# A decoder layer on one core: block 0's choice of experts ahead of the barrier, weight splits at other blocks, blocks turned a step ahead, last products ahead of row moments

## What is computed

```python
logits = x.astype(jnp.float32) @ gate_w.astype(jnp.float32).T
scores = jax.nn.softmax(logits, axis=-1)
topk_w, topk_idx = jax.lax.top_k(scores, K)
topk_w = topk_w / (topk_w.sum(-1, keepdims=True) + 1e-20) * RSF
capacity = math.ceil(CF * N * K / E)
pos = jnp.cumsum(one_hot, axis=0) - 1
...
eo = jnp.einsum('nei,ehi->neh', jax.nn.silu(g) * u, we_down)
y = jnp.einsum('neh,ne->nh', eo, comb)
sh = jax.nn.silu(x @ ws_gate.T) * (x @ ws_up.T) @ ws_down.T
```

## Time and profile before

| | |
|---|---|
| median of 3 runs | 1394.81 us (1392.65 to 1396.25) |
| profiled execution, its own time | 1398.77 us |
| its span | 1397.0 us |
| TensorE busy in the span | 1309.3 us (94%) |
| VectorE | 1078.8 us (77%) |
| ScalarE | 925.5 us (66%) |
| GpSimd | 456.2 us (33%) |
| mean granted TensorE clock | 0.975 |

### The profile page before, as it was taken

One profiled execution on the slowest core, in us unless ns is written; L12 is line 12 of the kernel. 1 busy time (PEld: TensorE's weight loads), 2 busy tenths in 40 slices (PEclk: granted clock), 3 DMA queues, 4 the chain that ended last, 5 costly groups with the idle time before them and its releaser, 6 DMA issues. The chain is left out here.

```text
span 1397.0 us, 27271 instructions
## 1 busy us (share of the span) xinstructions
PE 1309.3 (94%) x8312; PEld 776.9 (56%) x8312; DVE 1078.8 (77%) x2227; ACT 925.5 (66%) x1776; POOL 456.2 (33%) x487
## 2 busy tenths in 40 slices
PE   3999999999999999999999999999968999999995
PEld 2534454444444444444544445443546799999984
DVE  5889789888978887897898888889577745555566
ACT  3387767777777776776677677778655645565555
POOL 3334203301511330151133020111146636666662
PEclk8699999999999999999999999999999999999998
DMA  5554434334424433442443444242056447777694
GB/s 166 135 167 129 125 126 141 104 119 142 134 68 135 145 95 115 143 140 79 129 138 94 138 124 132 78 135 73 17 184 207 170 142 134 135 156 146 136 185 132
DMA packets 110089, 181.47 MB, mean 130 GB/s; under 512 B 20368, under 2 KB 67600, under 8 KB 105872
## 3 DMA queue, kind: packets, MB, share of 16 engines
q1 hardware_dynamic: 90576, 155.70, 36.6%
q0 software_dynamic: 18816, 23.60, 9.7%
q10 hardware_dynamic: 576, 0.79, 0.3%
HBM read 99.67 MB, written 79.30 MB: 128 GB/s over the span
## 5 line engine op out<-in xcount | busy, mean ns | idle before, releaser
L802 ACT ACTIVATE prob<-ps_sc 128x512 f32<-128x512 f32 x1024 | 551.3, 601 | 195.0 <-PE ps_sc L1064 194.1
L847 DVE TENSOR_REDUCE nm<-ps_ring 128x1 f32<-128x512 f32 x1024 | 638.5, 679 | 53.0 <-PE ps_ring L1049 52.5
L1049 PE MATMUL ps_ring<-qk 48*128 48x512 f32 x1024 | 408.6, 471 | 11.9 <-DMA qk<-hbm_self 7.1
L1064 PE MATMUL ps_sc<-qk 50*128 50x512 f32 x1024 | 389.8, 454 | 10.7 <-ACT prob L802 9.6
L1064 PEld LDWEIGHTS ps_sc<-qk 50*128 50x128 f32 x1024 | 161.5, 187 | 301.5 <-ACT prob L802 215.7
L1081 PE MATMUL ps_out<-prob,va 128*32 128x512 f32 x2048 | 276.8, 613 | 1.6 <-ACT ot L678 0.7
L1902 PE MATMUL ps_gu<-x2f,we 128*128 128x256 f32 (+1 forms) x1320 | 214.9, 317 | 3.2 <-ACT sg L1524 2.3
L1902 PEld LDWEIGHTS ps_gu<-x2f,we 128*128 128x128 f32 x1320 | 183.8, 191 | 17.1 <-ACT sg L1524 3.2
L1049 PEld LDWEIGHTS ps_ring<-qk 48*128 48x128 f32 x1024 | 167.1, 189 | 43.2 <-DVE nm L847 27.2
L1902 PE MATMUL ps_dn<-we,hf 128*128 128x256 f32 x864 | 115.6, 285 | 7.1 <-DVE hf L1766 7.1
L607 POOL TENSOR_TENSOR rstd<-mv,eps 128x2 f32<-128x2 f32 x32 | 6.3, 197 | 345.9 <-DVE mv L935 345.9
(11 more groups left out here) (182 smaller groups left out, 1578.6 us busy)
## 6 DMA issues: line engine op xcount, KB each, us to landing
qk<-hbm_cross SPq DMA_DIRECT2D x384, 64.0 KB, 2.3
qk<-hbm_self SPq DMA_DIRECT2D x372, 64.0 KB, 2.3
hbm_self<-stage SPq DMA_DIRECT2D x16, 1024.0 KB, 3.9
hbm_cross<-stage SPq DMA_DIRECT2D x16, 1024.0 KB, 4.1
slots_x<-zeros SPq DMA_DIRECT2D x8, 1360.0 KB, 5.9
xs<-slots_x SPq DMA_DIRECT2D x40, 272.0 KB, 3.2
weraw<-w_moe SPq DMA_DIRECT2D x11, 768.0 KB, 4.7
xin<-x SPq DMA_DIRECT2D x9, 512.0 KB, 4.0
```

The costliest lines, as they stand in the source:

```text
L802: nc.scalar.activation(prob[:, s % 2, j, :], ps_sc[:, score_bank(h.cur, HG * s + j), :], ACT.Exp, scale=HD ** -0.5).then_inc(exp_done[a], 1)
L847: nc.vector.tensor_reduce(nm[:, g % 2, r:r + 1], bank(slot), axis=AX.X, op=ALU.max, negate=True).then_inc(max_done[a], 1)
L1049: nc.tensor.matmul(bank(slot), qk[rows, 0, pair, P * c:P * c + P], qk[rows, 1, pair, :], start=True, stop=True).then_inc(smax_done[a], 1)
L1064: nc.tensor.matmul(ps_sc[:, score_bank(inst, n), :], qk[rows, 1, h // 2, P * c:P * c + P], qk[rows, 0, h // 2, :], start=True, stop=True). ...
```

## The change

1. Block 0's choice. `choose` becomes a function for both phases (`choose_experts`), and block 0's is called at the end of VectorE's list of the attention phase. For that, block 0's logits come from `first_score` at step 4 of `post`, into bank 3 of `ps_gu`, and are turned at step 8 into the same bank; `first_block(0, 0)` moves from step 4 to 8, `(0, 1)` from 8 to 10. ScalarE copies the logits at step 5, and makes the exponential at step 13, between two pairs of row normalisations. The second block's up product, `first_block(1, 1)`, needs bank 3 and waits for VectorE's read of it.
2. Weight splits. Splits 1, 2 and 3 (second shared expert, routed experts 0 and 1) stood at blocks 0 to 2 on ScalarE and 1 to 3 on VectorE. Now split 1 stands at block 5 on ScalarE and 6 on VectorE, splits 2 and 3 behind jobs 8 and 9. The loads of weights follow: number 3 behind block 6's store, numbers 4 and 5 behind the first chunk loads.
3. Turns. The first half of a block's turn is made a block sooner: block i+2 at the down products of block i-1, instead of block i+1 at the head of block i; `x_hi` and `x_lo` of that half move as well, ahead of the exponential and ahead of `choose`.
4. Tail. Moments 5 stand behind job 14 and moments 6 behind job 15's two products and low halves; normalisations 4 to 6 behind the silu of job 15.

The core of the diff:

```diff
+                    if h.name == "post" and s == 5:
+                        act.wait_ge(products_done, 1)
+                        nc.scalar.activation(by_expert[:, :], ps_gu[0:NE, 3, :], ACT.Copy).then_inc(kept_done, 1)
+                    if h.name == "post" and s == 13:
+                        act.wait_ge(shift_done, 1)
+                        nc.scalar.activation(r32[:, 1, :, :], r32[:, 0, :, :], ACT.Exp).then_inc(rexp_done, 1)
...
             every_period(dve, half)
+            choose_experts(dve, nc.vector, 0, ps_gu[:, 3, 0:TT * NE].rearrange("p (t e) -> p t e", t=TT), r4, r32, choice,
+                           idx[:, 0, :, :], sel, logits_done, shift_done, rexp_done, step_done)
...
                 if (c, kind) == (0, 0):
-                    pe.wait_ge(lo_done["c"], upto("c", GATE, 0))
-                    pe.wait_ge(lo_done["xt"], upto("xt", B, 1))
                     pe.wait_ge(exp_done[CROSS], B * NMAX)
-                    pe.wait_ge(oev_done[CROSS], B * NG)
+                if (c, kind) == (1, 1):
+                    pe.wait_ge(shift_done, 1)
...
                     if h.name == "post" and s == 4:
+                        first_score()
+                    if h.name == "post" and s == 8:
                         first_block(0, 0)
-                    if h.name == "post" and s == 8:
+                        first_logits()
+                    if h.name == "post" and s == 10:
                         first_block(0, 1)
-                    if h.name == "post" and s == 10:
                         first_block(1, 0)
                         first_block(1, 1)
-                        first_logits(owners)
...
-MOMENTS_AT = {(12, 0): 0, (12, 1): 1, (13, 0): 2, (13, 1): 3, (14, 0): 4, (15, 0): 5, (15, 1): 6}
-NORM_AT = {(12, 1): 0, (13, 0): 1, (13, 1): 2, (14, 0): 3, (14, 1): 4, (15, 1): 5}
+MOMENTS_AT = {(12, 0): 0, (12, 1): 1, (13, 0): 2, (13, 1): 3, (14, 0): 4, (14, 1): 5}
+NORM_AT = {(12, 1): 0, (13, 0): 1, (13, 1): 2, (14, 0): 3}
...
-                if i < 3:
-                    sp.wait_ge(w_lo, i + 2)
-                    load_weights(i + 3, EXPERTS[i + 3])
+                if i == 6:
+                    sp.wait_ge(w_lo, 2)
+                    load_weights(3, EXPERTS[3])
...
             for g in range(NCH - 1):
                 load_chunk(g, g)
+            for n in (4, 5):
+                sp.wait_ge(w_lo, n - 1)
+                load_weights(n, EXPERTS[n])
...
             for i in range(B):
-                if AHEAD <= i + 1 < B:
-                    x_hi(i + 1, 0)
                 gate(i, 0)
...
                 h_hi(i, 1)
+                if AHEAD <= i + 2 < B:
+                    x_hi(i + 2, 0)
...
-                if 1 <= i + 1 < 4:
-                    split_hi(i + 1, (i + 1) % 2, (i + 1) // 2 + 1)
+                if i == 5:
+                    split_hi(1, 1, 1)
 
             for j in range(B, LATE):
                 for c in range(IC):
                     gate(j, c)
                     h_hi(j, c)
                 keep(j - 1)
+                n = j - B + 2
+                split_hi(n, n % 2, n // 2 + 1)
...
+            for c in range(IC):
+                gate(NJ - 1, c)
+            norm(B - 4)
+            for c in range(IC):
+                h_hi(NJ - 1, c)
+            keep(NJ - 2)
+            norm(B - 3)
             norm(B - 2)
...
-                if 1 <= i < 4:
-                    split_lo(i, i % 2, i)
+                if i == 6:
+                    split_lo(1, 1, 1)
+                if AHEAD <= i + 2 < B:
+                    x_lo(i + 2, 0)
                 if i + 1 < B:
                     choose(i + 1)
...
+            for c in range(IC):
+                product(NJ - 1, c)
+            for c in range(IC):
+                h_lo(NJ - 1, c)
+            moments(B - 2)
             last_moments()
...
+            def turn_ahead(i):
+                pe.wait_ge(kept_done, i)
+                turn(i, 0)
...
             down(0)
+            turn_ahead(AHEAD)
             count(1)
...
                 down_pair(i - 1, 0)
+                if i + 2 < B:
+                    turn_ahead(i + 2)
                 if i + 1 < B:
                     turn_logits(i + 1)
                 down_pair(i - 1, 1)
```

More of the change, by code:

```diff
@@ L291, in attention_phase @@
     expert_rooms, block_rooms, raw_rooms = rooms
-    ident, wg, wgraw, idx, tok, spare, by_expert = held
-    gu_done, products_done, kept_done, logits_done = made
+    ident, wg, wgraw, idx, tok, spare, by_expert, r4, r32, choice, sel = held
+    gu_done, products_done, kept_done, logits_done, shift_done, rexp_done, step_done = made
     ps_gu, _, ps_t = banks
@@ L1194, in rooms_ahead, with wide, make_step, step @@
         return [ctx.enter_context(nc.sbuf_tensor(name, [P] + ROOMS[name], F32 if name == "weraw" else F32R)) for name in ROOMS]
+def wide(a):
+    return a.to_broadcast([P, TT, NE])
+def make_step(eng, step_done, i, done):
+    def step(ins):
+        done[0] += 1
+        ins.then_inc(step_done, 1)
+        eng.wait_ge(step_done, i * ROUTE_STEPS + done[0])
+    return step
+def choose_experts(eng, v, i, logits, r4, r32, choice, number, sel, logits_done, shift_done, rexp_done, step_done):
+    mx, total_e, inv, top1, j1, top2, j2 = (r4[:, k, :, :] for k in range(7))
+    shifted, e, s, eq, cand, rest = (r32[:, k, :, :] for k in range(6))
+    one, two = (choice[:, c, :, :] for c in range(2))
+    done = [0]
+    step = make_step(eng, step_done, i, done)
+    eng.wait_ge(logits_done, i + 1)
+    step(v.tensor_reduce(mx, logits, axis=AX.X, op=ALU.max))
+    v.tensor_tensor(shifted, logits, wide(mx), ALU.subtract).then_inc(shift_done, 1)
+    eng.wait_ge(rexp_done, i + 1)
+    step(v.tensor_reduce(total_e, e, axis=AX.X, op=ALU.add))
+    step(v.reciprocal(inv, total_e))
+    step(v.tensor_tensor(s, e, wide(inv), ALU.mult))
+    step(v.tensor_reduce(top1, s, axis=AX.X, op=ALU.max))
+    step(v.tensor_tensor(eq, s, wide(top1), ALU.is_equal))
+    step(v.tensor_tensor(cand, eq, number, ALU.mult))
+    step(v.tensor_reduce(j1, cand, axis=AX.X, op=ALU.min))
+    step(v.tensor_tensor(one, number, wide(j1), ALU.is_equal))
+    step(v.scalar_tensor_tensor(out=rest, in0=one, scalar=-2.0, in1=s, op0=ALU.mult, op1=ALU.add))
+    step(v.tensor_reduce(top2, rest, axis=AX.X, op=ALU.max))
+    step(v.tensor_tensor(eq, rest, wide(top2), ALU.is_equal))
+    step(v.tensor_tensor(cand, eq, number, ALU.mult))
+    step(v.tensor_reduce(j2, cand, axis=AX.X, op=ALU.min))
+    step(v.tensor_tensor(two, number, wide(j2), ALU.is_equal))
+    step(v.tensor_tensor(sel[:, 0:TT, :], one, two, ALU.add))
+    assert done[0] == SELECTED, done
 def moe_phase(nc, x2, slots_x, sums, w_moe, out, x2_out, rooms, banks, held, made):
@@ L1230, in moe_phase @@
         shift = sb("shift", [P, 2, TT, 1])
-        r4 = sb("r4", [P, 8, TT, 1])
-        r32 = sb("r32", [P, 9, TT, NE])
-        choice = sb("choice", [P, 2, TT, NE])
         prod = sb("prod", [P, 2, TT, NE])
@@ L1635, in _ @@
             weigh(CHUNKS - 2, 0, NCH - 2, NE - 1)
-            for j in range(LATE, NJ):
+            for j in range(LATE, NJ - 1):
                 for c in range(IC):
@@ L1725, in take_counts @@
             def take_counts(i):
-                step = make_step(i, [CHOSEN])
+                step = make_step(dve, step_done, i, [CHOSEN])
                 dve.wait_ge(cnt_done, i + 1)
@@ L1735, in place @@
                 q, done = i % HELD, [CHOSEN + 1]
-                step = make_step(i, done)
+                step = make_step(dve, step_done, i, done)
                 step(v.tensor_scalar(past, pos, float(CAP), float(PLACES), ALU.is_ge, ALU.mult))
@@ L1988, in _ @@
             for i in range(2, B):
-                if i + 1 < B:
-                    turn(i + 1, 0)
                 gate_up(i, 0)
```

70 lines of the change are left out of this document (20 added, 50 removed).

## The result

The changed kernel takes 1381.61 us (median of 4 runs, 1381.40 to 1384.98), the kernel before 1395.53 us in the runs beside it (1392.65 to 1397.15): a ratio of 0.9908, 95% interval 0.9891 to 0.9925. So it is faster by some 12.8 us by the ratio (the two medians are 13.9 apart), and the 1381.6 lie 1.2 us under the predicted 1382.8. The profiled execution is the longest of the four, 1384.98 us with a span of 1383.2 us.

A forecast was written before the change was run, and what follows sets the result against it. VectorE's serial loop was taken to bound the blocks and tail, TensorE the routed part. Terms -7.0 (entry to block 2), -4.6, +2.0, +1.4 and -4.0 sum to -12.2 us: 1382.6 from the median 1394.81, stated as 1382.8, range 1379 to 1388.

The forecast's parts named there:

- The likeliest case: Whole kernel: the terms hold as summed, giving 1382.8 us; chance 0.72.
- the clock under 1 in block 2: TensorE in block 2: a granted clock under 1 there would show the prediction wrong; the fall had cost 2.0 us before.
- Entry: Barrier to block 1: barrier opens 0.8 us later, block 1's choice is done 1.4 early; with block 1's wait, -0.5 us.
- Wait at block 1: TensorE's queue: block 3's turn, ahead of block 1's count, waits for ScalarE's logits copy; of 1.4 us won, 0.5 is left.
- Block 2: Block 2: the 7.74 us wait becomes waits of 1.6 and 2.3, the clock recovers 2.0 us; -6.5 us.
- Blocks 3 to 6: Blocks 3 to 6: splits leave VectorE's loop, 11.7 us a block, 46.8 instead of 51.4; -4.6 us.
- Block 7: Block 7: the split staying ahead of its choice makes the count wait some 1.9 us; +2.0 us.
- Routed start: First routed chunk: the last split, queued right ahead on ScalarE and VectorE, makes TensorE wait 1.3 us; +1.4 us.
- Tail: End of the routed part: moments fill VectorE's idle time, two products and low halves run together; -4.0 us.
- Rival B: Partial gain: the clock falls behind short waits, rows come late, or the tail gives back half; about 1387 us, chance 0.17.
- Rival C: No change that can be told: tail keeps its length and routed start waits 4 us; 1393 us, chance 0.07.
- rival D: Slower: the last split's weights (routed expert 1) land late, slowing the kernel only from 28 us; 1400 us, chance 0.04.

The follow-up runs named there:

- reduce_more: The changed kernel with one more VectorE operation, a row maximum written to unread room, in blocks 1 to 5; ratio 0.9920 to the kernel before.
- after_again: The changed kernel itself, unaltered, run again as control beside kernels made from it; 1382.94 us, ratio 0.9909 to the kernel before.
- no_choice: The changed kernel with block 0's choice put back behind the barrier, other three parts kept; ratio 0.9924 to the kernel before.
- count_first: The changed kernel with block 3's first half turn put behind block 1's count in TensorE's queue; 1380.97 us, ratio 0.9900 to the kernel before.
- both: The changed kernel with block 3's turn behind block 1's count and weight splits 2 and 3 one place earlier; 1382.33 us, ratio 0.9900.
- splits_again: The kernel before with only the weight splits and their loads moved, second run; ratio 0.9964 to the kernel before.
- turns_again: The kernel before with only the half turns made a step ahead, second run; ratio 0.9965 to the kernel before.

## Why the prediction was right

**The mechanism** was the one named: VectorE's loop, a long wait in block 2, and a tail on VectorE alone. The likeliest case came out, and three of the signs were there: the barrier set by VectorE, the longest wait in the blocks under 3 us and on the choice in block 2, and no idle time of VectorE behind the sixth moments. None of TensorE's turns waited for a load of rows. Two signs were not as given: the wait at the first chunk was 0.42 us, or 0.75 with the wait for its load, and not 1 to 1.5, and the clock under 1 in block 2, by which I would be wrong, is absent in the first profile and in reduce_more but there in after_again, no_choice, count_first and both.

**Entry**, -0.5: measured 0.0, the term with the wrong size. The barrier opened 1.0 us later by TensorE's first product (16.5 us behind the fixed point instead of 15.5; predicted 0.8), and the first product of VectorE came 2.3 us earlier (predicted 1.5): ScalarE, which I had waiting 1.25 us behind the barrier for GpSimd, started its table load at once (1017.78). But the clock behind the barrier took 1.2 to 1.3 us of it. I had looked at that clock only in block 2, and TensorE's wait of 2.79 us at the barrier is not among the four waits that I listed. With the clock at 1.00 there, in after_again, count 1 came 1.3 us sooner.

**Wait at block 1**, predicted as a loss of 0.9 out of 1.4 us. Moving the count ahead of it (count_first) brings count 1 forward by 2.2 us and the routed start by 1.5. So I named the wait and its cause, and made its price too small. (After_again is what this is held against; its clock was full up to block 2's count.)

**Block 2**, -6.5: measured -5.5. Entry and block 2 together miss 1.5 us of the 7.0 predicted. Of these, 0.9 is that the counts of block 1 were taken later (33.0 us behind the fixed point, predicted 36.1 less the fixed point's 4.1), and 0.5 is the rest of the block: from the counts to its end I had 16.2 us, and it took 16.7 (1034.25 to 1050.94). The two waits in it were right, 1.43 and 2.17 us where 1.6 and 2.3 stood, and so was the return of the clock in that execution. That return is luck of the execution: in after_again block 2 takes 17.00 us (1034.16 to 1051.16), 4.4 less than before and not 5.5.

**Blocks 3 to 6**, -4.6: measured -4.15, 11.82 us a block where 11.7 stood. The parts of it are confirmed alone: 12.0 without splits (splits_again), 0.2 less with the turns (turns_again). That VectorE sets them holds, with an addition: reduce_more shows that 0.2 us of its loop is ScalarE's reply, and after_again shows TensorE doing a block in 11.41 us, as my sum of its starts had it. So the next saving on VectorE would be worth at most 0.4 us a block.

**Block 7**, +2.0: +1.85. **Routed start**, +1.4: +1.2, in another make-up. The low half cost 0.7 (1.02 us from the last transposes to the products, before 0.36) and not 1.3, and the load of the first chunk, which I had not looked at, the other 0.5.

**Tail**, -4.0: -4.2, and between -3.8 and -4.4 over all seven profiles with that order, -4.17 of them alone.

**Sum.** By stage the terms make -11.0 against a predicted -12.2, and the ratio -12.8 (-15.2 to -10.5 by the interval). The 1382.8 lay 1.2 us from the median. What of that is luck can be told: the terms were 1.2 us too good, and a share of 1.8 us which the stages don't show made up for it, the attention's noise (below) or something that the profiled execution had not. The working has three small slips on which nothing hangs: 33.1+0.7+0.5+0.5+0.6 is 35.4 and not 35.5, eight scatters of 1.04 with 0.3 between are 10.7 and not 10.3, and 1382.6 was put down as 1382.8 without a reason.

**The four parts don't add up quite.** At the routed start, alone, the splits are worth 4.1, the turns 3.6, the choice 0.7: 8.4 in sum. Together they give 6.6 and 7.4 in the two profiles, and 9.0 with the count first. Why is not shown. The turn's place ahead of count 1 can't be the whole reason, for turns_again has it too; the splits and the turns both shorten the one wait of 7.74 us, by 2.4 and 6.2, which is more than there is; and the clock fell at another place in each execution. At the end of the kernel the difference is gone: from the fixed point on, the parts alone give 3.8 (splits), 3.2 (turns), -0.45 (choice) and 4.2 (tail), 10.7 in sum, and the two profiles of the whole 11.0 and 11.2. Between the two places lies the wait of the first total's moments for their load, which is 0.3 us in the first profile and 0.5 to 1.5 in these others.

**Rival B** was right in a part. Behind short waits the clock falls in every profile of the changed kernel and of its variants, each time for 1.1 to 1.6 us of TensorE's time, but not always at the place where I had looked: behind the barrier (the first profile, both, reduce_more), in block 2's first products (count_first, no_choice, and turns_again), or behind block 2's count (after_again, both, and turns_again). The Trainium skill, "TensorE: Matmul & The Clock Gate", part 1, says that the throttled state is the default and that activity releases it; I had read that as several short waits doing what the long one did, 2.0 us worse. The traces agree in part: 1.1 us in after_again's block 2, 0 in the first profile's. Rival C and rival D did not come; no weights were late.

## What to carry to other kernels

When a loop waits on one engine, cost each part of its serial queue by starts, and ask at once how far the next engine is from being the bound: here 4.2 us came from four blocks which at 11.8 us stand 0.4 above TensorE's own 11.4, so that little more is to be had there. When a step is moved ahead, look at what it is moved in front of: a turn that waits 1.5 us in front of a count of 0.3 us held up that count by 2.2 us, of which 1.5 were still there at the routed start. Where a profile's own time stands 3 to 4 us from the median, compare stages from a common instruction behind the part that varies, and not the spans.

## What the runs showed of the hardware that was not expected

**TensorE's clock falls without a long wait.** The attention is the same in the kernel before and in splits_again, but takes 1004.09 us in the one profile and 996.65 in the other. TensorE's windows from 300 to 360 us, before and then splits_again:

```profile
300.00:360.00 60.00, 58.56 (x349) 27.57 (x351) 49.80 (x95) 42.42 (x83) 10.48 (x14) 0.94 0.42 127
```

```profile
300.00:360.00 60.00, 58.58 (x368) 28.35 (x368) 53.32 (x101) 44.22 (x87) 12.41 (x15) 1.00 0.42 130
```

TensorE is busy 58.6 of 60 us in both, but the granted clock is 0.94 and 1.00, and in the first 349 matmuls are done instead of 368. Such dips stand in other windows in other executions. Over the windows from 60 to 960 us the clock missing from 1.00 adds up to some 10 us before and 2 in splits_again, about the 7.4 us between them. It fits the distance of 3 to 4 us between a profile and its median. Inside the dip before the clock is at the lower of its levels:

```profile
344.00:345.00 1.00, 1.00 (x8) 0.50 (x4) 0.56 (x2) 0.17 (x1) 0.00 (x0) 0.50 0.04 8
```

What sets the dips off stays open. In the five microseconds ahead of this one TensorE waited 0.19 and 0.41 us; at the same instructions splits_again waited 0.20 and 0.39, and its clock stayed at 1.00.

**The place where the clock falls behind short waits is not fixed.** Two executions of the same kernel with the same waits (2.79 us at the barrier, 2.1 to 2.2 at block 2's count) paid in different places, 1.3 us in the one and 1.1 in the other. Of the 1.1 in block 2, 0.5 was left at count 7.

**Engines stopped with nothing to wait for.** In one set of runs all four kernels with a trace had stops of 1 to 4 us, on one or more of TensorE, VectorE and ScalarE, between block 1 and the routed part. The kernel before was as slow beside them (1407.96 us instead of 1395), though no trace of it from that set shows the stops. On the same chip a while later they were gone. I found no cause; whether the engines waited for their own program was not tested.
